# Gated cross-attention and ternary FFN on one core: three weight matrices loaded by GpSimd without DRAM copies

## The reference, cut to what matters

```python
x = x + tanh(g_xattn[0]) * xattn(layernorm(x), ctx, ctx, Wh, wg_w, wo_w, gamma, beta)
x = x + tanh(g_ffn[0]) * ffn(layernorm(x), gate_w, up_w, down_w, gate_s, up_s, down_s)
# x, ctx: (64, 128, 512); Wh: (4, 128, 128); gate_w, up_w: (1408, 512); down_w: (512, 1408)
def xattn(x, k, v, Wh, wg_w, wo_w, gamma, beta):
    Q, K, V = [einsum('bshd,hde->bshe', t, Wh) for t in (x, k, v)]     # 4 heads of 128
    masked = einsum('bshe,bthe->bhst', Q, K) / sqrt(128) * decay
    A = maximum(abs(masked.sum(axis=0)), 1.0)                          # summed over the batch
    O = einsum('hst,bthe->bshe', A, V)
    return relu(x @ wg_w) * (normalized(O) * gamma + beta) @ wo_w
def ffn(x, gate_w, up_w, down_w, gate_s, up_s, down_s):
    h = silu((x @ gate_w.T) * gate_s) * ((x @ up_w.T) * up_s)
    return (h @ down_w.T) * down_s
```

## Time and profile before

| | us |
|---|---|
| median of 3 runs | 1511.12 |
| the 3 runs | 1510.38, 1511.45, 1511.12 |
| span of the profiled execution | 1510.4 |
| TensorE (PE) busy in it | 1492.9 |
| VectorE (DVE) busy | 1059.0 |
| GpSimd (POOL) busy | 719.3 |
| ScalarE (ACT) busy | 680.1 |

### The profile page before, as it was taken

The page is one execution under the profiler, slowest core; times in us unless marked ns, Lnnn a source line. Parts: engine busy times, 40 slices in busy tenths (PEclk is TensorE's granted clock), DMA queues, the critical chain, the costliest instruction groups (busy, mean ns, idle before and its releaser), DMA issues.

```text
span 1510.4 us, 20333 instructions
## 1 busy us (share of the span) xinstructions
PE 1492.9 (99%) x7226; PEld 1254.7 (83%) x7226; DVE 1059.0 (70%) x1501; ACT 680.1 (45%) x1063; POOL 719.3 (48%) x767
## 2 busy tenths in 40 slices
PE   7999999999999999999999999999999999999998
PEld 5888888888888888888888888888888888888887
DVE  7777778788566676666677667564777778778672
ACT  4444444445545535555354544534344344443442
POOL 5456666762453445445453544434138237237236
PEclk9999999999999999999999999999999999999999
DMA  7888878875787686777877787676373472562422
GB/s 227 296 265 274 265 268 286 265 232 203 223 248 230 198 243 209 191 236 205 244 219 198 228 230 235 170 213 157 115 216 105 138 213 99 140 202 95 144 94 85
DMA packets 374663, 305.94 MB, mean 203 GB/s; under 512 B 258400, under 2 KB 284384, under 8 KB 374368
## 3 DMA queue, kind: packets, MB, share of 16 engines
q1 hardware_dynamic: 374560, 304.61, 67.1%
HBM read 200.23 MB, written 117.31 MB: 210 GB/s over the span
## 4 chain that ended last, share of the span: by engine, by line
PE 91%; POOL 3%; DVE 3%; DMA 2%; issue 1%; ACT 1%; SPq 0%; POOLq 0%; DVEq 0%; ACTq 0%
PE ps L1743 42%; PE po L1743 8%; PE pyb L1622 8%; PE ptb L1743 5%; PE pyb L1743 5%; PE po L1622 5%; PE ps L1657 5%; PE pyb L1727 4%; PE ptb L1727 4%; PE ptb L1731 2%; PE pyb L1731 2%; PE ptb L1627 1%; PE ps L1622 1%; DMA v_scratch<-tmp 1%; POOL reg L1493 1%; POOL sums L1515 1%
## 5 line engine op out<-in xcount | busy, mean ns | idle before, releaser
L1448 POOL TENSOR_SCALAR rs<-mv 128x1 f32<-128x1 f32 (+1 forms) x132 | 52.7, 399 | 284.2 <-DVE mv L1079 144.3
L1622 PE MATMUL pyb<-reg,xreg 128*128 128x512 f32 x708 | 178.0, 398 | 2.2 <-DVE reg L971 2.2
L1540 POOL TENSOR_TENSOR reg<-tmp,reg 128x512 fp32r<-128x512 f32 x88 | 118.1, 1342 | 125.1 <-ACT reg L743 125.1
L1743 PE MATMUL ps<-reg,gate 128*128 128x512 f32 x704 | 174.7, 390 | 0.6 <-DVE tmp L1205 0.6
L1743 PE MATMUL ps<-reg,up 128*128 128x512 f32 x704 | 173.9, 389 | 0.0
L1743 PE MATMUL ps<-op,wbuf 128*128 128x512 f32 x704 | 173.9, 389 | 0.0
L1743 PE MATMUL ps<-xreg,reg 128*128 128x512 f32 x704 | 163.1, 389 | 0.0
L1520 POOL TENSOR_TENSOR p5b<-p5b,p1b 128x512 f32<-128x512 f32 x44 | 57.1, 1299 | 216.0 <-ACT p5b L767 216.0
L1743 PEld LDWEIGHTS ps<-op,wbuf 128*128 128x128 f32 x704 | 132.1, 188 | 27.4
L1743 PEld LDWEIGHTS ps<-reg,up 128*128 128x128 f32 x704 | 132.1, 188 | 27.4
L1743 PEld LDWEIGHTS ps<-xreg,reg 128*128 128x128 f32 x704 | 131.6, 188 | 27.4 <-POOL reg L1540 0.4
(11 more groups left out here) (154 smaller groups left out, 2822.2 us busy)
## 6 DMA issues: line engine op xcount, KB each, us to landing
wbuf<-ws_scratch SPq DMA_DIRECT2D x44, 896.0 KB, 4.9
xr<-in_x SPq DMA_DIRECT2D x62, 512.0 KB, 5.7
raw<-in_ctx_t SPq DMA_DIRECT2D x32, 512.0 KB, 4.7
w_scratch<-tmp SPq DMA_DIRECT2D x64, 256.0 KB, 5.1
v_scratch<-tmp SPq DMA_DIRECT2D x64, 256.0 KB, 4.3
raw<-v_scratch SPq DMA_DIRECT2D x32, 512.0 KB, 6.8
x_scratch<-xr SPq DMA_DIRECT2D x32, 512.0 KB, 4.6
xr<-x_scratch SPq DMA_DIRECT2D x32, 512.0 KB, 5.9
```

What stands on the lines that cost most here:

```text
L1540: e.tensor_tensor(hid[1][:, m % 11, :], tmp[:, m % 3, :], f(hid[0][:, m % 11, :]), ALU.subtract).then_inc(s["hlo"])
L1622: last = e.matmul(dst, lhs[a], rhs[b], start=(k == 0 and i == 0), stop=(k == n - 1 and i == 2))
L1743: last = e.matmul(dst, l, r, start=(k == 0 and i == 0), stop=(k == n - 1 and i == 1), skip_group_check=sums)
```

## The change

SP no longer issues the 12 copies to DRAM, the 8 loads of gate and up chunks and the 4 loads of down, and the three scratch tensors and their semaphores are gone. POOL issues 8 loads of gate and up chunks straight from the inputs (`weights_load`, 704 KB each, one at the start of each of its passes 1 to 8) and 11 loads of down (`down_load`, 256 KB each, at steps 2 to 5 of the FFN's first group: 3, 3, 3 and 2). The six copies of weights into `ws_scratch` later on read the inputs in place of the scratch.

```diff
-        xreg = sb("xreg", [128, NI * 512], f32r)
+        xreg = placed("xreg", [128, NI * 512], f32r)
+        gate32, up32 = gate, up
+        down32 = xreg[:, 0:NI * 512].rearrange("p (i n) -> p i n", i=NI)
...
-        chunks = ([(src[128 * k:128 * k + 128, :], copy[128 * k:128 * k + 128, :], dst[:, k, :])
-                   for first in range(2)
-                   for src, copy, dst in ((gate_t, gate_s, gate), (up_t, up_s, up))
-                   for k in (first, first + 2)]
-                  + [(down_t[352 * k:352 * k + 352, :], down_s[352 * k:352 * k + 352, :], None) for k in range(4)])
+        chunks = [(src[128 * k:128 * k + 128, :], dst[:, k, :])
+                  for first in range(2)
+                  for src, dst in ((gate_t, gate32), (up_t, up32))
+                  for k in (first, first + 2)]
...
             for g in range(1, NG):
                 more = g + 1 < NG
-                if g < 12:
-                    weights_chunk(g)
-                if g <= 8:
-                    p.wait_ge(f"scr{(g - 1) % 2}", 16 * ((g - 1) // 2 + 1))
-                    p.wait_ge(f"wld{(g - 1) % 2}", 16 * ((g - 1) // 2))
-                    _, src, dst = chunks[g - 1]
-                    e.dma_start(f(dst), src).then_inc(s[f"wld{(g - 1) % 2}"], 16)
...
-                    if g == 0 and 2 <= step < 6:
-                        down_load(step - 2)
...
+            def weights_load(n):
+                if n >= 2:
+                    p.wait_ge(f"wld{n % 2}", 16 * (n // 2))
+                src, dst = chunks[n]
+                e.dma_start(dst, src.bitcast(f32r)).then_inc(s[f"wld{n % 2}"], 16)
+
+            def down_load(i):
+                if i == 0:
+                    p.wait_ge("w", B)
+                    p.wait_ge("v", B)
+                    p.wait_ge("ad", 1)
+                e.dma_start(down32[:, i, :], down_t[128 * i:128 * i + 128, :].bitcast(f32r)).then_inc(s["dld"], 16)
...
                 if g == 0:
                     rstd(5)
+                elif g <= 8:
+                    weights_load(g - 1)
                 ct_split(g + 1, 0)
...
+                    if g == 0 and 2 <= step < 6:
+                        for i in range(3 * step - 6, min(3 * step - 3, NI)):
+                            down_load(i)
...
-                    p.wait_ge("dld", 64)
+                    p.wait_ge("dld", 16 * NI)
```

More of the change, by code:

```diff
@@ L17 @@
     + ["wys", "wyl", "x2s", "x2l"]
-    + ["scr0", "scr1", "wld0", "wld1"]
+    + ["wld0", "wld1"]
     + ["ones", "eps", "rs", "rs2", "cthi", "ctlo", "sadd", "p15"]
@@ L193, in gated_layer @@
         w_s = nc.dram_tensor("w_scratch", [NG, 128, 4, 512], f32, kind="Internal").ap()
-        gate_s = nc.dram_tensor("gate_scratch", [D, INTER], f32, kind="Internal").ap()
-        up_s = nc.dram_tensor("up_scratch", [D, INTER], f32, kind="Internal").ap()
-        down_s = nc.dram_tensor("down_scratch", [INTER, D], f32, kind="Internal").ap()
         wy_s = nc.dram_tensor("wy_scratch", [2, 128, D], f32, kind="Internal").ap()
@@ L307, in ct_load @@
                             ct_v[:, 2 * hp:2 * hp + 2, 512 * g:512 * g + 512]).then_inc(s[f"ct{hp}"], 16)
[L309 to L313, removed]
             def v_store(t):
@@ L350, in w_load @@
                 e.dma_start(wt_of(q), w_s[q // 2, :, :, 256 * (q % 2):256 * (q % 2) + 256]).then_inc(s[f"wl{q % 2}"], 16)
[L352 to L361, removed]
             def x_again(q):
@@ L407, in weights_copy @@
             def weights_copy(o, k):
-                src, row = {G1: (gate_s, 0), G2: (gate_s, 256), U2: (up_s, 256)}[o]
+                src, row = {G1: (gate_t, 0), G2: (gate_t, 256), U2: (up_t, 256)}[o]
                 e.dma_start(ws_s[:, :, k, o, :].rearrange("j p n -> p j n"),
@@ L478, in _ @@
             v_store(1)
-            weights_chunk(0)
             v_store(2)
@@ L1007, in low_weights @@
                     p.wait_ge(f"wld{c % 2}", 16 * (c // 2 + 1))
-                    low_bits(chunks[c][2][:, 704 * half:704 * half + 704], "and")
+                    low_bits(chunks[c][1][:, 704 * half:704 * half + 704], "and")
                 else:
```

## The result

| | before | after |
|---|---|---|
| median, us (runs of one chip) | 1511.28 | 1531.53 |
| lowest and highest | 1510.38, 1511.81 | 1530.70, 1532.54 |
| span of the profiled execution | 1510.4 | 1528.9 |
| TensorE busy in it | 1492.9 | 1495.2 |

The ratio is 1.0133, with an interval of 1.0121 to 1.0146: the change costs 20.25 us where 20.5 were forecast.

What follows compares the result with a forecast made beforehand. TensorE, busy in 1492.9 of 1510.4 us, was taken to bound the kernel. A stall of 20.4 plus 1.7 for the clock less a gain of 1.6 made 20.5 us, so 1511.1 + 20.5 = 1531.6 us, range 1509 to 1546.

Steps and rivals of the forecast that it cites:

- The held issues: At the FFN, each POOL issue waits for its previous transfer's landing, delaying `wy_pair_lo`; TensorE stalls 20.4 us; chance 0.57.
- TensorE's clock: Behind the FFN stall, TensorE is granted a clock of 0.57 for 4 us, losing 1.7 us.
- The gain in the first stage: The pass behind SP's copy of down and load of up gets back its whole 1.64 us, booked as -1.6.
- The prediction's own case for no gain: In that first-stage pass, the gain could be nothing if the remaining store of sums sets the landing alone.
- The sum: All terms together, 20.5 us, added to the median of 1511.1 us for 1531.6 us.
- POOL in the first stage: Eight 704 KB loads, one a pass, cost 0, as the slack of 5.9 us covers each issue.
- The last two loads: At the FFN, they hold back only the `hidden_lo` behind them; booked as nothing, at most 4.3 us.
- What lies around the span: For the whole kernel, the span of 1510.4 us was taken as 0.7 below the median of the runs.
- Cheap issues: Rival at POOL's loads: issues cost up to 1.08 us, POOL is never held, only the gain remains; 1509.5 us, chance 0.22.
- A hold by DVE: Rival at POOL's FFN issues: each waits for one DVE instruction, 1.87 us per issue; stall 7.1, 1518.3 us, chance 0.15.
- An issue held until its own landing: Rival, both stages: every issue holds POOL until its transfer lands; 14.4 us first stage, 29.0 FFN; 1554.6 us, chance 0.06.

Runs made afterwards that it cites:

- down_back: Against the change: gate and up stay on POOL, down goes through its DRAM scratch and SP as before; 1511.67 us, ratio 1.0002.
- one_pool: Against the kernel before: only the last tile of down loaded by POOL, at step 5 of the first FFN group; 1510.92 us, ratio 0.9999.
- weights_back: Against the kernel before: gate and up still through the scratch by SP, the eleven loads of down by POOL; 1531.27 us, ratio 1.0133.
- late448: Against the change: 448 bytes for descriptors, down loads three at step 2, three at 5, three at 7, two at 8; 1515.57 us, ratio 1.0028.
- ring1024: Against the change: 1024 bytes in place of 256 for the descriptors of POOL's transfers, nothing else; 1514.07 us, ratio 1.0013.
- spread: Against the change: one load of down at each of the steps 0 to 10, still 256 bytes; 1524.08 us, ratio 1.0085.
- ring448: Against the change: 448 bytes in place of 256 for the descriptors of POOL's transfers, nothing else; 1515.86 us, ratio 1.0029.
- late1024: Against the change: 1024 bytes for descriptors, the last four down loads moved to step 6, behind `wy_pair_lo`; 1511.46 us, ratio 1.0000.

## Why the prediction was right, step by step

**The held issues** (predicted: 8 landings of 4.3 us, a stall of 20.4; measured 18.7). The mechanism is the one that was forecast: the room for descriptors decides, which the four kernels with 256 to 1024 bytes show; that a held issue waits for the last landing and not for the oldest makes no difference with room for one. The product came at 431.7 us and not at 435.1. Of these 3.4 us, 1.8 are no error of the step: in this execution the FFN began 1.8 us earlier, and TensorE's need with it (414.66 - 1.83 = 412.83). Most of the other part is the spacing, 4.14 us from issue to issue in place of 4.3, 8 x 0.16 = 1.3 us. That 4.3 came so close is partly luck. It was SP's median for a store; these loads have a median of 3.4 us and a mean of 3.80 over the first eight, drawn up by the first two (6.37 and 4.91), and on top come 0.31 us from a landing to the next issue, which the prediction left out. In the stretch, the first matmul that uses the product starts 18.73 us later than before. 17.87 of it is the wait; 0.69 had been lost just ahead, 0.37 of it in a wait for ACT at line 702, and the remaining 0.17 is not broken down.

**TensorE's clock** (predicted 1.7, measured 1.60). The stretch at the start of the kernel was a good stand-in, though its wait was 2.16 us and this one 17.87.

**The gain in the first stage** (predicted -1.6). This is the step that failed. The value products on both sides of that pass after, which answer to the earlier trace rows:

```profile
190.45 3.15 PE L1645 MATMUL ps<-reg 128*128 128x256 f32 x24
...
212.80 3.10 PE L1645 MATMUL ps<-reg 128*128 128x256 f32 x24
```

The pass takes 212.80 - 190.45 = 22.35 us against 22.83, so 0.5 us came back, and even that is within what such passes vary by. Over this pass and the one ahead of it together, the three kernels that keep the copy of down (before, down_back, one_pool) take 44.23 to 44.82 us, and the nine without it 43.58 to 45.05; the means are 44.56 and 44.36. So the gain is about 0.2 us. Taken alone, that pass is 22.45 to 22.83 us long with the copy and 22.35 to 22.93 in the eight kernels that have no copy and let POOL issue the load of up. The ninth without the copy is weights_back, where SP issues that load as before: 21.79 us, the shortest of the twelve, with no wait of TensorE over 0.15 us in it. So taking the copy away may have brought up to 1.0 us there, and the load's move to POOL may have taken it back; that is one execution, and what delays the pass stays open. The prediction's own case for no gain was the store of sums, which stays; weights_back has it too and the short pass, so it is not the store alone. The medians alone could not tell 1.6 us from nothing, as the interval of the change is 1.9 us wide to either side.

**The sum** was right by two errors that cancel. The forecast was 20.4 + 1.7 - 1.6 = 20.5. The stretch gives 18.7 + 1.6 = 20.3 in place of 22.1, and the gain is 0.2 in place of 1.6: 20.1, beside the measured 20.25.

**POOL in the first stage** (predicted 0). Right within 1.4 us, by down_back: the issues take 0.66 us and the loads land in 5.0 us in the median, with 42 us to the next use of their semaphore. Open is only the pass above, 21.79 us in weights_back.

**The last two loads** (predicted 0, at most 4.3). Right: the tenth was issued at 431.66 and the eleventh at 435.56, and TensorE waits for nothing up to the product with down. late448 shows that this was not safe by much: two loads held there until 438.60 cost 5.5 us in its profile.

**What lies around the span.** The prediction took the span of 1510.4 for the time of that execution. Every run here is 1.8 us longer than its span, so the profiled execution of before took about 1512.2 us, some 0.9 above the median. It cancels, since the sum was carried over to the median as a difference.

**The rivals.** Cheap issues are out by the wait of 17.9 us. A hold by DVE is out by the spacing, 4.14 us and not 1.87, by its change with the room for descriptors, and by the ninth load: POOL sat idle 2.72 us until 427.61, while DVE did nothing from 425 to 430 (the stretch above). An issue held until its own landing is out by the third load of a triple: it is over at 406.90, and `hidden_lo` starts at 406.92.

## What to carry to other kernels

An issue by GpSimd is cheap in itself (0.53 to 0.67 us) as long as its descriptors find room; the first that does not fit holds the engine until all transfers ahead of it have landed, and all that is queued behind it there. Count the transfers that fit, put no more than these ahead of an instruction that TensorE waits for, do not count on room coming back with each landing, and check the last load against its own deadline too. Taking away traffic and waits that nothing critical waited for bought no measurable time here, though 8.65 MB fewer went through the scratch.

## What the runs showed of the hardware

- Transfers of 128 partitions that POOL issues before one is held: 1, 2, 3 and 7 with 256, 320, 448 and 1024 bytes. The profile puts the hold down to "issue" or, at times, to an engine that had long been done.
- A held issue starts 0.3 to 0.4 us after the last transfer ahead of it has landed (53 of 53), also where the oldest landed long before: 401.5 against 411.26 us in ring1024.
- The median landing of a 256 KB load was 3.4 us (the change) and 4.3 (spread) with one under way, 4.3 with up to two, 5.8 and 6.0 with up to three (ring448, late448), 7.6 and 8.1 with up to six (ring1024, late1024). At 128 KB with one under way it was 2.4, only 1.0 us less than in the change.
- A wait of TensorE of 2.02 us in ring1024 was followed by a granted clock of 0.65 for 4 us, and the stretch became 3.95 us longer; in ring448, behind one of 1.72 us, the clock stayed at 1.00 and the stretch grew by 2.06. The stretches behind the waits, ring1024 and then ring448 (columns as in the earlier trace rows):

```profile
415.98:419.98 4.00, 3.99 (x12) 3.17 (x13) 0.00 (x0) 1.17 (x3) 3.52 (x4) 0.65 0.90 263
```

```profile
416.10:420.10 4.00, 3.91 (x17) 3.24 (x18) 0.00 (x0) 0.12 (x1) 1.97 (x4) 1.00 0.89 284
```

  TensorE does 12 matmuls in the one and 17 in the other. Between these two executions, one of each kernel, 0.3 us more of waiting went with 1.9 us more of stretch.
